# Adapter factors of the first network's gate and up: sums by single sequences inside tile 1, rows spread through DRAM

## The chip, the cores and the metric

The kernel runs on one core of a Trainium2 chip. Its time is the device time of one launch in microseconds; lower is better. The profile is of one execution.

## The reference

Tokens x are 8 sequences of 128 tokens with 512 features, all in float32. Each sequence picks its own low-rank adapters (rank 16) by an index. Cut to what matters:

```python
# first network
gate = x @ W_gate.T + (x @ A_gate[ids].T) @ B_gate[ids].T * 0.5     # 512 -> 1376
up   = x @ W_up.T   + (x @ A_up[ids].T)   @ B_up[ids].T   * 0.5
act  = silu(gate) * up
cond = act @ W_down.T + (act @ A_down[ids].T) @ B_down[ids].T * 0.5  # 1376 -> 512
x = x + ffn0(cond)      # 512 -> 1792 -> 512, weights w * (su @ sv) of rank 4
# second network
y = x @ W.T + b + (x @ A1[ids1]) @ B1[ids1] * 2
x = x + ffn1(y)         # 512 -> 1792 -> 512, int4 weights with scales
```

The change concerns the products x @ A_gate[ids].T and x @ A_up[ids].T, called t below: for each sequence 16 gate rows and 16 up rows of 128 tokens.

## The kernel before, in words

Features lie on the 128 partitions; HK = 4 blocks of 128 features make up 512, and the 1024 tokens are two chunks c of 512 (CH = 2), each of four sequences. A float32 operand is split into a rounded high part (ScalarE, `_hi`) and the rest (VectorE, `lo`), and each block product is three matmuls of 128 x 512: high by high, high by low, low by high (`sums`, L2355 to L2357). The gate/up weights of the first network come in 11 tiles of 128 outputs. Tiles 0 and 1 are computed plainly (`plain_base(t, c)`: gate bank, then up bank, 12 matmuls each), tiles from 2 on with seven products over sums of blocks.

Every engine has its program written out in one order, tied together by semaphores. `first_tiles` is TensorE's start: 12 warm-up matmuls (`WARM`, L2783), tile 0 in both chunks, the adapter sums, tile 1 in both chunks, and then the adapter products of both tiles (`gate_up_adapters`, L2365), followed by the tiles from 2 on.

The adapter sums (L2374) work on pairs of sequences: for each chunk and block, four matmuls of 32 weight columns by 256 tokens, one on each quarter of the array's columns (two pairs for gate, two for up). Their weights are the factors of two sequences side by side, reordered on ScalarE from a_gu_raw into a_gu (L1578). Half of each result belongs to the wrong sequence; VectorE multiplies by seg_mask to clear it (L2221, into gated). ScalarE writes the high part into quarter 0 of t_rows (`hi_of_t`), VectorE the low part into quarter 2 (`lo_of_t`), and SP copies each to the quarter behind it inside SBUF (`copy_t`, L863 and L865; semaphore t_copied). t_rows then has four quarters of 32 rows (high, high, low, low), and one matmul against b_rows (the B factors as high, low, high, low) adds the adapters to a tile.

b_rows comes by DMA through DRAM: SP stores the split B factors (`store_first`, L802, into b_split) and spreads them with four transfers per group of tiles (`spread_b`, L810). spread_b(0) serves tiles 0 and 1, spread_b(1) tiles 2 and 3. SP also issues nearly all weight loads in its fixed order: after x come the adapter factors of four sequences, tile 1's weights (load(gu_a, 1), L781), B factors, load(gu_a, 2), down factors, store_first(0), copy_t(0), spread_b(0), copy_t(1), store_first(1), load(gu_a, 3), spread_b(1). GpSimd issues the loads of the other four sequences, then waits, and later computes the block sums of tile 3 (`cond_sums(3)`, L1026 on).

Of the kernel before, what the change touches and what calls it, by code (L numbers as in the profile page):

```python
# [6 lines left out]
F32 = mybir.dt.float32  # L7
F32R = mybir.dt.float32r
# [57 lines left out]
WARM = 12  # L66
# [127 lines left out]
def adaln_ffn(nc, d, out):  # L194
# [7 lines left out]
    with ExitStack() as ctx:  # L202
# [116 lines left out]

        gate_sum = place("gate_sum", [P, 4, TOK], F32, at["h"])  # L320
# [19 lines left out]
        a_gu = place("a_gu", [P, HK, 2, NB, R], F32, at["act_lo"] + 8 * KB)  # L340
# [35 lines left out]
        a_gu_ready = sem("a_gu_ready")  # L376
# [3 lines left out]
        t_copied = [sem(f"t_copied{c}") for c in range(CH)]  # L380
# [164 lines left out]


# [83 lines left out]
        start = [("w", 0)] + [("x", 0, k) for k in range(HK)] + [("w", 1)] + [("x", 1, k) for k in range(HK)]  # L630
# [130 lines left out]

        block = ctx.enter_context(nc.Block())
# [3 lines left out]
        def _(sp):  # L766
# [60 lines left out]

            for n, item in enumerate(start):
# [8 lines left out]

            sp.wait_ge(ids_in[0], 16)
            indices = {b: sequence(sp, b) for b in range(BC, NB)}
            for b in range(BC, NB):  # L840
                load_a_gu(sp, b, indices[b])
            gu_a, down_a, gu_b, down_b, gu_c, down_c = phases[:6]
            load(gu_a, 1)
            for b in range(BC, NB):
                load_b(sp, b, indices[b], 0, b_in[b // BC])
# [14 lines left out]
            def copy_t(c):  # L860

                sp.wait_ge(t_hi_rows, c + 1)
                sp.dma_start(t_rows[quarter(1), :, chunk(c)].bitcast(F32), t_rows[quarter(0), :, chunk(c)].bitcast(F32)).then_inc(t_copied[c], 16)  # L863
                sp.wait_ge(t_lo_rows_done, c + 1)
                sp.dma_start(t_rows[quarter(3), :, chunk(c)].bitcast(F32), t_rows[quarter(2), :, chunk(c)].bitcast(F32)).then_inc(t_copied[c], 16)  # L865

            store_first(0)
            copy_t(0)
            sp.wait_ge(b_stored[0], 16 * 2)
            spread_b(0)  # L870
            copy_t(1)
# [126 lines left out]
        def _(pool):  # L998
# [12 lines left out]
            for b in range(BC):  # L1011
                load_a_gu(pool, b, indices[b])
            for b in range(BC):
                load_b(pool, b, indices[b], 0, b_in[b // BC])
            pool.wait_ge(start_lo, len(start))
            for b in range(BC):
                load_a_dn(pool, b, indices[b])

# [180 lines left out]
        def _(act):  # L1199
# [44 lines left out]
            def hi_of_t(c, nets):  # L1244

                n = nets * RB
                act.wait_ge(t_masked, (0 if nets == 2 else CH + 1) + c + 1)
# [308 lines left out]
            def small_t(ph):  # L1556
# [4 lines left out]
                for c in range(CH):  # L1561
                    hi_of_t(c, 1)
# [22 lines left out]
            for c in range(CH):  # L1585
                hi_of_t(c, 2)
# [1341 lines left out]
```

## Time and profile before

| what | value |
|---|---|
| median of 3 runs | 606.76 us (606.46 to 607.78) |
| profiled execution | 606.15 us, span 604.5 us |
| TensorE busy | 99% of the span, 2904 matmuls |
| VectorE, ScalarE, GpSimd busy | 78%, 49%, 48% |
| DMA | 56.06 MB, mean 93 GB/s |

The span runs from the first to the last instruction; the runs are some 1.6 us longer than the span. PE is TensorE (PEld its weight loads), DVE is VectorE, ACT ScalarE, POOL GpSimd, SPq the queue of SP, which issues DMAs. In a timeline a line gives the start, the time covered, engine, line of the kernel, operation, what is written from what, the shape and how many instructions are merged; in brackets stands the idle time ahead of it and what ended it. Matmul ends are modelled and overlap the next start; the distance of starts is the pace.

### The profile page before, as it was taken

How to read it: one execution, taken by the hardware profiler on the slowest of the kernel's cores; microseconds unless marked ns; L12 is line 12 of the kernel's file. 1: busy time of each engine (PE TensorE's matmuls, PEld its weight loads, DVE VectorE, ACT ScalarE, POOL GpSimd, SP SyncE). 2: the span in 40 equal slices, each digit the busy share in tenths (PEclk: the TensorE clock that was granted, in tenths of full speed). 3: DMA queues.
4: the chain of work that ended last, by engine and by line, in shares of the span. 5: the costliest groups of instructions: out<-in, count | busy, mean ns of one | idle time of the engine just before them, and what ended most of it. 6: DMA issues, size and time to landing. Idle time of an engine off the chain costs nothing.

```text
span 604.5 us, 8075 instructions
## 1 busy us (share of the span) xinstructions
PE 599.7 (99%) x2904; PEld 491.9 (81%) x2904; DVE 469.7 (78%) x572; ACT 295.3 (49%) x413; POOL 292.7 (48%) x219
## 2 busy tenths in 40 slices
PE   8999999999999999999999999999999999999997
PEld 7787887878778888888888878888788888888886
DVE  6797757757778999873459877645879998999987
ACT  5865224323443445441124445334658886478860
POOL 6135334324434055831034586520005889958897
PEclk9999999999999999999999999999999999999999
DMA  8896472541171215212121200342232221322203
GB/s 255 220 227 180 148 170 65 131 130 28 53 207 37 71 35 166 69 31 66 35 71 35 70 30 31 84 83 84 61 101 78 77 69 36 109 67 75 75 7 139
DMA packets 30475, 56.06 MB, mean 93 GB/s; under 512 B 10468, under 2 KB 14532, under 8 KB 30052
## 3 DMA queue, kind: packets, MB, share of 16 engines
q1 hardware_dynamic: 28932, 53.05, 30.7%
q0 software_dynamic: 1216, 1.98, 1.5%
q8 instruction: 23, 0.38, 0.3%
q10 hardware_dynamic: 288, 0.52, 0.2%
q14 instruction: 16, 0.13, 0.1%
HBM read 48.44 MB, written 6.06 MB: 90 GB/s over the span
## 4 chain that ended last, share of the span: by engine, by line
PE 99%; DVE 0%; issue 0%
PE ps_down L2355 7%; PE ps_down L2356 7%; PE ps_down L2357 7%; PE ps_gate L2458 3%; PE ps_gate L2639 3%; PE ps_gate L2638 3%; PE ps_up L2638 3%; PE ps_gate L2459 3%; PE ps_gate L2460 3%; PE ps_up L2639 3%; PE ps_m L2638 3%; PE ps_down L2638 3%; PE ps_m L2639 3%; PE ps_down L2639 3%; PE ps_up L2458 3%; PE ps_up L2459 2%
## 5 line engine op out<-in xcount | busy, mean ns | idle before, releaser
L1144 POOL TENSOR_TENSOR up_sum<-up_sum,up_more 128x1024 f32<-128x1024 f32 x14 | 33.7, 2409 | 62.6 <-DVE up_more L1926 62.6
L2355 PE MATMUL ps_down<-act_hi,w_hi 128*128 128x512 f32 x112 | 43.9, 392 | 0.0
L2356 PE MATMUL ps_down<-act_lo,w_hi 128*128 128x512 f32 x112 | 43.6, 390 | 0.0
L2357 PE MATMUL ps_down<-act_hi,w_lo 128*128 128x512 f32 x112 | 43.6, 389 | 0.0
L1026 POOL TENSOR_TENSOR cond_total<-w_raw 128x512 f32<-128x512 f32 x8 | 10.5, 1310 | 60.4 <-DMA w_raw<-in_cond_gu 36.3
L1691 DVE TENSOR_TENSOR w_lo<-w_total,w_hi 128x512 fp32r<-128x512 f32 (+1 forms) x28 | 28.8, 1030 | 13.3 <-ACT w_hi L1462 12.6
L1926 DVE SCALAR_TENSOR_TENSOR gate_sum<-ps_up,s_group,gate_sum 128x1024 f32<-128x1024 f32 x28 | 35.8, 1279 | 3.8 <-PE ps_up L2639 3.7
L1102 POOL TENSOR_TENSOR act_lo<-up,act_hi 128x512 fp32r<-128x512 f32 x14 | 18.1, 1295 | 39.1 <-ACT act_hi L1468 39.1
L1156 POOL TENSOR_TENSOR act_lo<-gate_sum,act_hi 128x1024 fp32r<-128x1024 f32 x14 | 33.7, 2413 | 6.3 <-DVE gate_sum L1934 6.3
L1462 ACT ACTIVATE w_hi<-w_total 128x512 fp32r<-128x512 f32 (+1 forms) x28 | 20.7, 738 | 28.8 <-POOL w_total L1089 19.4
L1036 POOL TENSOR_TENSOR act_lo<-cond_out,act_hi 128x512 fp32r<-128x512 f32 (+1 forms) x14 | 19.1, 1389 | 28.9 <-ACT act_hi L1303 28.9
L2181 DVE TENSOR_TENSOR xp<-xp,ps_down 128x512 f32<-128x512 f32 x16 | 11.0, 685 | 27.4 <-PE ps_down L2357 27.4
L2458 PE MATMUL ps_gate<-x_hi,w_hi 128*128 128x512 f32 x80 | 31.9, 398 | 0.0
L2459 PE MATMUL ps_gate<-x_lo,w_hi 128*128 128x512 f32 x80 | 31.2, 390 | 0.0
L2460 PE MATMUL ps_gate<-x_hi,w_lo 128*128 128x512 f32 x80 | 31.2, 390 | 0.0
L1084 POOL TENSOR_TENSOR w_total<-w_raw 128x512 f32<-128x512 f32 x7 | 9.5, 1354 | 42.9 <-DVE w_raw L1698 33.6
L1151 POOL TENSOR_TENSOR gate_sum<-gate_sum,up_sum 128x512 f32<-128x512 f32 (+1 forms) x14 | 20.4, 1459 | 11.7 <-ACT gate_sum L1382 11.7
L2458 PE MATMUL ps_up<-x_hi,w_hi 128*128 128x512 f32 x66 | 26.0, 394 | 0.0
L2459 PE MATMUL ps_up<-x_lo,w_hi 128*128 128x512 f32 x66 | 25.8, 390 | 0.0
L2460 PE MATMUL ps_up<-x_hi,w_lo 128*128 128x512 f32 x66 | 25.7, 389 | 0.0
L2357 PEld LDWEIGHTS ps_down<-act_hi,w_lo 128*128 128x128 f32 x112 | 21.0, 188 | 4.5
L2355 PEld LDWEIGHTS ps_down<-act_hi,w_hi 128*128 128x128 f32 x112 | 21.0, 188 | 4.3
(413 smaller groups left out, 2031.5 us busy)
## 6 DMA issues: line engine op xcount, KB each, us to landing
w_int<-in_ffn_gu SPq DMA_DIRECT2D x14, 512.0 KB, 3.5
w_raw<-in_ffn_gu SPq DMA_DIRECT2D x10, 512.0 KB, 4.1
w_raw<-in_cond_gu SPq DMA_DIRECT2D x9, 512.0 KB, 5.9
w_raw<-in_ffn_dn SPq DMA_DIRECT2D x8, 448.0 KB, 3.2
w_int<-in_ffn_dn SPq DMA_DIRECT2D x8, 448.0 KB, 3.2
b_rows<-b_split SPq DMA_DIRECT2D x12, 256.0 KB, 4.6
xp<-in_x SPq DMA_DIRECT2D x8, 256.0 KB, 4.9
w_raw_third<-in_ffn_gu SPq DMA_DIRECT2D x4, 512.0 KB, 4.0
```

The lines of the kernel that those rows point to most:

```text
L1144: nc.gpsimd.tensor_tensor(up_sum[:, u % 3, :], up_sum[:, u % 3, :], up_more[:, u % 2, :], ALU.add).then_inc(up_done, 1)
L1156: nc.gpsimd.tensor_tensor(act_lo[:, j, :], gate_sum[:, u % 4, :], act_hi[:, j, :].bitcast(F32), ALU.subtract).then_inc(unit_ready, 1)
L1691: return nc.vector.tensor_tensor(out_, value, hi.bitcast(F32), ALU.subtract)
L1926: return nc.vector.scalar_tensor_tensor(out=here, in0=group_bank(g), scalar=group_scale(g), in1=here, op0=ALU.mult, op1=ALU.add)
L2355: nc.tensor.matmul(ps[:, :], weights_hi[:, cols], rhs_hi(k), start=start and n == 0, stop=False)
L2356: nc.tensor.matmul(ps[:, :], weights_hi[:, cols], rhs_lo(k), start=False, stop=False)
L2357: last = nc.tensor.matmul(ps[:, :], weights_lo[:, cols], rhs_hi(k), start=False, stop=stop and n == len(ks) - 1)
L2458: nc.tensor.matmul(bank[:, :], w7_hi[s][:, cols], x_hi[n][:, k, :], start=not more and k == 0, stop=False, skip_group_check=more)
L2459: nc.tensor.matmul(bank[:, :], w7_hi[s][:, cols], x_lo[n][:, k, :], start=False, stop=False, skip_group_check=more)
L2460: last = nc.tensor.matmul(bank[:, :], w7_lo[s][:, cols], x_hi[n][:, k, :], start=False, stop=k == 1, skip_group_check=more)
L2638: nc.tensor.matmul(bank[:, chunk(c)], weights, hi[:, chunk(c)], start=True, stop=False)
L2639: last = nc.tensor.matmul(bank[:, chunk(c)], weights, lo[:, chunk(c)], start=False, stop=True)
```

## The change

In words:
- The sums go by single sequences: four matmuls of 32 weight columns (16 gate, 16 up) by 128 tokens for each chunk and block, read from a_gu_raw as loaded. The reordering a_gu, the mask product on gated and the writes into t_rows by ScalarE and VectorE go for this use.
- The sums stand in tile 1, between the gate and the up bank of chunk 0 (`between`).
- ScalarE takes the high part of a whole result (128 x 128) and VectorE the low part. GpSimd stores the high halves to DRAM (t_split) and spreads them with 8 transfers of 16 partitions into t_rows; SP does the same with the low halves, its 8 transfers behind spread_b(0). VectorE clears t_rows at the start, since the transfers write only each sequence's own places. All adapter products wait for all 16 transfers.
- Tile 0's first chunk alternates gate and up by block, and the up weights are loaded third, not sixth. Nine warm-up matmuls, not twelve.
- Tile 1's weights are loaded ahead of the adapter factors, and the B factors ahead of the A factors.
- On ScalarE and VectorE the x sums for tile 2 (`cond_x_high`, `cond_x_sum`) change places with the work around them. Some semaphore counts of later stages shift, with no work changed there.

```diff
-WARM = 12
+WARM = 9
...
+        t_first_hi, t_first_lo = (place(f"t_first_{part}", [P, CH, P], F32R, at[home]) for part, home in (("hi", "t_hi"), ("lo", "gated")))
+        t_split = nc.dram_tensor("t_split", (2, NB, 2, R, P), F32, kind="Internal").ap()
...
-        start = [("w", 0)] + [("x", 0, k) for k in range(HK)] + [("w", 1)] + [("x", 1, k) for k in range(HK)]
+        start = [("w", 0), ("x", 0, 0), ("w", 1)] + [("x", 0, k) for k in range(1, HK)] + [("x", 1, k) for k in range(HK)]
...
+        def store_t(eng, half, c):
+
+            value = (t_first_hi, t_first_lo)[half][:, c, :]
+            eng.dma_start(t_split[half, c * BC:(c + 1) * BC].rearrange("s g r n -> (s g r) n"), value.bitcast(F32)).then_inc(t_stored[half], 16)
+
+        def spread_t(eng, half):
+
+            for q in (2 * half, 2 * half + 1):
+                for odd in range(2):
+                    rows = t_rows[q * PR + odd * R:q * PR + (odd + 1) * R, :, :].rearrange("r g (p e n) -> r g p e n", e=2, n=P)
+                    values = t_split[half].rearrange("(p e) g r n -> e g r p n", e=2)[odd]
+                    for g in range(2):
+                        eng.dma_start(rows[:, g, :, odd, :].bitcast(F32), values[g]).then_inc(t_copied[half], 16)
...
+            load(gu_a, 1)
             sp.wait_ge(ids_in[0], 16)
             indices = {b: sequence(sp, b) for b in range(BC, NB)}
             for b in range(BC, NB):
+                load_b(sp, b, indices[b], 0, b_in[b // BC])
+            for b in range(BC, NB):
                 load_a_gu(sp, b, indices[b])
-            gu_a, down_a, gu_b, down_b, gu_c, down_c = phases[:6]
-            load(gu_a, 1)
-            for b in range(BC, NB):
-                load_b(sp, b, indices[b], 0, b_in[b // BC])
...
-            def copy_t(c):
-
-                sp.wait_ge(t_hi_rows, c + 1)
-                sp.dma_start(t_rows[quarter(1), :, chunk(c)].bitcast(F32), t_rows[quarter(0), :, chunk(c)].bitcast(F32)).then_inc(t_copied[c], 16)
-                sp.wait_ge(t_lo_rows_done, c + 1)
-                sp.dma_start(t_rows[quarter(3), :, chunk(c)].bitcast(F32), t_rows[quarter(2), :, chunk(c)].bitcast(F32)).then_inc(t_copied[c], 16)
-
             store_first(0)
-            copy_t(0)
+            for c in range(CH):
+                sp.wait_ge(t_first_lo_done, c + 1)
+                store_t(sp, 1, c)
             sp.wait_ge(b_stored[0], 16 * 2)
             spread_b(0)
-            copy_t(1)
+            sp.wait_ge(t_zero, 1)
+            sp.wait_ge(t_stored[1], 16 * CH)
+            spread_t(sp, 1)
...
+                load_b(pool, b, indices[b], 0, b_in[b // BC])
+            for b in range(BC):
                 load_a_gu(pool, b, indices[b])
-            for b in range(BC):
-                load_b(pool, b, indices[b], 0, b_in[b // BC])
             pool.wait_ge(start_lo, len(start))
             for b in range(BC):
                 load_a_dn(pool, b, indices[b])
+
+            for c in range(CH):
+                pool.wait_ge(t_first_hi_done, c + 1)
+                store_t(pool, 0, c)
+            pool.wait_ge(t_zero, 1)
+            pool.wait_ge(t_stored[0], 16 * CH)
+            spread_t(pool, 0)
...
-            def hi_of_t(c, nets):
-
-                n = nets * RB
-                act.wait_ge(t_masked, (0 if nets == 2 else CH + 1) + c + 1)
-                nc.scalar.activation(t_hi[0:n, c, 0:PT], gated[0:n, c, 0:PT], ACT.Copy).then_inc(t_hi_done, 1)
-                for g in range(nets):
-                    for half in range(2):
-                        for row in (0, 1) if nets == 1 else (0,):
-                            last = nc.scalar.activation(t_rows[quarter(row), g, pair_tokens(2 * c + half)],
-                                                        gated[quarter(2 * g + half), c, 0:PT], ACT.Copy)
+            def hi_of_first_t(c):
+
+                act.wait_ge(t_sums, c + 1)
+                nc.scalar.activation(t_first_hi[:, c, :], ps_m[:, sample_sums(c)], ACT.Copy, scale=0.5).then_inc(t_first_hi_done, 1)
...
-                act.wait_ge(a_gu_in[c], 16 * BC)
-                for g in range(2):
-                    nc.scalar.activation(a_gu[:, :, g, c * BC:(c + 1) * BC, :], a_gu_raw[:, c * BC:(c + 1) * BC, :].rearrange(
-                        "p b (k g r) -> p g k b r", g=2, r=R)[:, g], ACT.Copy).then_inc(a_gu_ready, 1)
...
-            cond_x_high(3)
+            for n in (3, 1):
+                cond_x_high(n)
             for c in range(CH):
-                hi_of_t(c, 2)
-            for n in (1, 4):
-                cond_x_high(n)
+                hi_of_first_t(c)
+            cond_x_high(4)
...
+            def lo_of_first_t(c):
+
+                dve.wait_ge(t_first_hi_done, c + 1)
+                nc.vector.scalar_tensor_tensor(out=t_first_lo[:, c, :], in0=ps_m[:, sample_sums(c)], scalar=0.5, in1=t_first_hi[:, c, :].bitcast(F32),
+                                               op0=ALU.mult, op1=ALU.subtract).then_inc(t_first_lo_done, 1)
...
+            nc.vector.memset(t_rows[:, :, :].bitcast(F32), 0.0).then_inc(t_zero, 1)
...
-            for n in (3, 1, 4):
-                cond_x_sum(n)
+            cond_x_sum(3)
             dve.wait_ge(w_hi_done, 1)
             lo(plain_lo[1][:, :], w_raw[:, 1, :], plain_hi[1][:, :]).then_inc(w_ready, 1)
             for n in range(2):
                 lo_of_b_first(n)
-            dve.wait_ge(mask_ready, 4)
+            for n in (1, 4):
+                cond_x_sum(n)
             for c in range(CH):
-                dve.wait_ge(t_sums, c + 1)
-                nc.vector.scalar_tensor_tensor(out=gated[:, c, 0:PT], in0=ps_m[:, pair_sums(c)], scalar=0.5, in1=seg_mask[:, :],
-                                               op0=ALU.mult, op1=ALU.mult).then_inc(t_masked, 1)
-                lo_of_t(c, 2)
+                lo_of_first_t(c)
...
-                pe.wait_ge(t_copied[c], 16 * 2)
+                for half in range(2):
+                    pe.wait_ge(t_copied[half], 16 * 8)
...
+                if (t, c) == (0, 0):
+                    for k in range(HK):
+                        for g in range(2):
+                            last = part(g, range(k, k + 1))
+                else:
+                    for g in range(2):
+                        last = part(g, range(HK))
+                        if g == 0:
+                            between()
...
+            def first_t():
+
+                for c in range(CH):
+                    pe.wait_ge(a_gu_in[c], 16 * BC)
+                    for k in range(HK):
+                        for q in range(4):
+                            sample = BC * c + q
+                            last = nc.tensor.matmul(ps_m[quarter(q), sample_sums(c)], a_gu_raw[:, sample, k * 2 * R:(k + 1) * 2 * R],
+                                                    xp[:, k, sample * P:(sample + 1) * P], start=k == 0, stop=k == HK - 1)
+                    last.then_inc(t_sums, 1)
+
             def first_tiles():
 
                 for c in range(CH):
                     plain_base(0, c)
-                for c in range(CH):
-                    pe.wait_ge(a_gu_ready, 2 * (c + 1))
-                    for k in range(HK):
-                        last = pair_products(c, lambda q: pair_factors(a_gu[:, k, q // 2], c, q), lambda q: xp[:, k, pair_tokens(2 * c + q % 2)],
-                                             k == 0, k == HK - 1)
-                    last.then_inc(t_sums, 1)
                 pe.wait_ge(w_ready, 1)
-                plain_base(1, 0)
-                pe.wait_ge(t_masked, CH)
+                plain_base(1, 0, first_t)
+                pe.wait_ge(t_first_lo_done, CH)
```

## Rows read from the trace of the kernel before

**Rows 1.** Page, busy time, and the chain that ended last by engine.

```profile
PE 599.7 (99%) x2904; PEld 491.9 (81%) x2904; DVE 469.7 (78%) x572; ACT 295.3 (49%) x413; POOL 292.7 (48%) x219
...
PE 99%; DVE 0%; issue 0%
```

**Rows 2.** All waits of TensorE over the span: total us, times, longest.

```profile
PE ps_m L2783 <- DVE warm L2203: 1.7, 1, 1.7
```

**Rows 3.** Timeline of TensorE, 0 to 45 us: start, us, work.

```profile
1.65 5.49 PE L2783 MATMUL ps_m<-warm 128*128 128x512 f32 x12 [1.65 <-DVE warm L2203]
6.94 0.63 PE L2355 MATMUL ps_down<-h_hi,plain_hi 128*128 128x512 f32 x1
...
7.80 0.43 PE L2357 MATMUL ps_down<-h_hi,plain_lo 128*128 128x512 f32 x1
8.06 0.39 PE L2355 MATMUL ps_down<-h_hi,plain_hi 128*128 128x512 f32 x1
...
18.36 3.66 PE L2374 MATMUL ps_m<-xp,a_gu 128*32 128x256 f32 x64
21.95 0.50 PE L2355 MATMUL ps_gate<-h_hi,plain_hi 128*128 128x512 f32 x1
...
32.96 0.64 PE L2365 MATMUL ps_down<-t_rows,b_rows 128*128 128x256 f32 x4
...
43.06 0.40 PE L2365 MATMUL ps_down<-t_rows,b_rows 128*128 128x256 f32 x2
```

**Rows 4.** Timeline of VectorE, 0 to 60 us.

```profile
1.11 0.48 DVE L2203 MEMSET warm<- 128x512 f32 x1 [1.11 <-PEq L2921]
4.29 0.78 DVE L1691 TENSOR_TENSOR plain_lo<-w_raw,plain_hi 128x512 fp32r<-128x512 f32 x1 [2.69 <-ACT plain_hi L1570]
5.19 0.69 DVE L1691 TENSOR_TENSOR h_lo<-xp,h_hi 128x512 fp32r<-128x512 f32 x1
6.83 2.03 DVE L1691 TENSOR_TENSOR h_lo<-xp,h_hi 128x512 fp32r<-128x512 f32 x3 [0.95 <-ACT h_hi L1574]
...
18.38 1.23 DVE L1691 TENSOR_TENSOR plain_lo<-w_raw,plain_hi 128x1024 fp32r<-128x1024 f32 x1 [1.96 <-ACT plain_hi L1581]
```

**Rows 5.** Timeline of ScalarE, 0 to 45 us.

```profile
15.14 1.34 ACT L1578 ACTIVATE a_gu<-a_gu_raw 128x256 f32<-128x256 f32 x4 [2.86 <-DMA a_gu_raw<-in_a_gu]
...
21.39 0.42 ACT L1248 ACTIVATE t_hi<-gated 128x256 fp32r<-128x256 f32 x1 [0.23 <-DVE gated L2221]
```

**Rows 6.** The sums' weight loads by line: duration ns min/median/max.

```profile
L2374 PEld LDWEIGHTS ps_m<-xp,a_gu x64: 106/110/110, 18.4 to 21.4; 128*32 128x32 f32 x64
```

**Rows 7.** Timeline of SP's DMA queue, 0 to 60 us: issues.

```profile
10.54 0.43 SPq L781 DMA_DIRECT2D w_raw<-in_cond_gu  x1
...
24.88 2.02 SPq L810 DMA_DIRECT2D b_rows<-b_split  x4
...
27.59 0.59 SPq L865 DMA_DIRECT2D t_rows<-t_rows  x1
...
29.34 0.48 SPq L781 DMA_DIRECT2D w_raw<-in_cond_gu  x1
34.07 1.74 SPq L810 DMA_DIRECT2D b_rows<-b_split  x4
```

**Rows 8.** Tile t_rows, its four DMA copies, issue to landing.

```profile
DMA to landing us min/median/max: 2.3/3.8/5.4
```

**Rows 9.** DMA issues, 0 to 60 us and whole span: KB, us to landing.

```profile
factor_split<-factor_lo SPq DMA_DIRECT2D x3, 36.0 KB, 1.8
...
b_raw<-in_b POOLq DMA_DIRECT2D x8, 32.0 KB, 2.7
```

**Rows 10.** Timeline of GpSimd, 0 to 70 us.

```profile
35.50 1.29 POOL L1026 TENSOR_TENSOR cond_total<-w_raw 128x512 f32<-128x512 f32 x1 [16.75 <-DMA w_raw<-in_cond_gu]
...
38.69 1.94 POOL L760 DMA_DIRECT2D b_raw<-in_b  x4
```

**Rows 11.** Window 23 to 25 us: busy by engine, PEclk, DMA share, GB/s.

```profile
23.00:25.00 2.00, 2.00 (x10) 1.67 (x9) 1.46 (x5) 1.35 (x4) 0.00 (x0) 1.00 0.14 43
```

## What I predict, before the change was run

> **What bounds the kernel now.** I read the page first. TensorE is busy for 99% of the span, and the chain that ended last runs through it for 99% [rows 1]. The list of waits, asked for TensorE alone, has one entry: the 1.7 us before the warm-up matmuls [rows 2]. So no wait can be taken away here. The time falls only if TensorE gets less to do, or does real work where it warms up, and every gap that a change opens in its queue is paid in full. The next view is the timeline of each engine over the first 45 us, because the diff touches nothing later but semaphore counts. Twelve warm-up matmuls begin at 1.65 us, the first real one starts at 6.94, the adapter sums run from 18.36 to 21.95, the adapter products of tiles 0 and 1 start at 32.96, and tile 2's at 43.06 [rows 3]. From 21.95 to 32.96 lie 48 matmuls, so one costs 0.229 us. The matmul at 7.80 still takes 0.43 us and the one at 8.06 is at full pace, so TensorE runs at 1.2 GHz up to about 7.85 us, after 6.2 us of unbroken work, and at 2.4 GHz from there (granted clock 1.00 in a later window [rows 11]). The number that decides the case is 32.96 and what it becomes.
>
> **Part 1, the start.** VectorE has the first block of x split at 5.19 + 0.69 = 5.88 us [rows 4], but TensorE is still warming up until 6.94. Nine warm-up matmuls of 0.44 end at 5.6, so real work starts at 5.95 (I take 0.06 for a semaphore, as between the end of the memset, 1.11 + 0.48, and 1.65 [rows 3, 4]). Three matmuls at half pace end at 7.2. The next three need the up weights, which now are the third load. Today's third load is x's second block, the same 256 KB, and VectorE starts on its split at 6.83 [rows 4], so the up weights are ready at 7.5 and TensorE goes on at 7.6. The clock should rise near 7.85 as before; it has then done 4 matmuls, not 2.5. The remaining 44 of tile 0 at 0.229 end at 18.0, against 18.3: a gain of 0.3 us. The later x blocks come 0.7 us apart, each feeding 1.4 us of work, so none is late. The new memset of t_rows is four times the old one, at most 4 x 0.48 = 1.9 us from 1.6 on, and VectorE's next work is later than 3.5 [rows 4]: nothing.
>
> **Part 2, the sums.** Today 64 matmuls take 3.59 us: 16 rounds of four column quarters, 0.22 each [rows 3]. The new ones have half the columns, which gives 0.11 a round; a 32-column weight load takes 0.11 too [rows 6]. So 0.11 to 0.12 a round, 1.9 us in all with its two joints; the upper bound is that the round stays at 0.22 and nothing is gained. I take 1.9 (both parts of a round halve or fit), a gain of 1.7. The mask product, the four fp32 reorderings on ScalarE (15.14, 1.34 us [rows 5]) and the eight 32-row copies go; the engines that did them are off the path, so this counts only through readiness.
>
> **Part 3, the order.** Tile 1's gate half now runs ahead of the sums, from 18.0 to 20.7. Its weights are split at 18.38 + 1.23 = 19.6 today [rows 4], which would be a stall of 1.6 us; but the load now goes out right behind the x loads and not at 10.54 [rows 7]. Eight splits of 0.7 after 6.83 keep VectorE to about 13, one x sum and the split itself follow, so it is ready near 15.4. The adapter factors are issued some 2 us later than today, when ScalarE had them at 15.14 [rows 5]; they have until 20.8. Both at nothing. The sums then run 20.8 to 22.7, and 36 matmuls (the up half and the second chunk) of 8.25 us follow: TensorE reaches the adapter products at 30.95. That is 2.0 us before 32.96, and is the most that the change can give.
>
> **Part 4, the rows.** Today SP copies t_rows inside SBUF, the last copy issued at 27.59 [rows 7]; with up to 5.4 us to land [rows 8] it is there at 33.0, just as TensorE arrives. The new way has two transfers in a row for each half, and every TensorE use waits for all of both. I add up the high half, which goes through GpSimd:
> 1. second chunk's sums readable at 22.8, ScalarE 0.3 (0.42 for 256 elements [rows 5]): 23.2.
> 2. store of 64 KB. Bounds: 1.8 us to land for SP's stores of 36 KB, 5.4 for the t_rows copies among other traffic [rows 8, 9]; GpSimd's loads of 32 KB take 2.7 [rows 9]. I take 2.8: 26.0.
> 3. eight issues. GpSimd's four of 16 partitions take 1.94, so 0.49 each [rows 10]; the eighth starts at 26.0 + 7 x 0.49 = 29.5.
> 4. its landing, 2.7 by the row of 32 KB, with 0.7 added because SP's rows are in flight: 3.4, so 32.9. Bounds 1.8 and 5.4.
> The low half goes through SP: VectorE has it at 23.45, the stores are out at 23.9, then spread_b(0) with four issues of 2.02 in all [rows 7] keeps SP until 25.9, the stores have landed by 26.3, eight issues at about 0.47 (the b_rows issues' pitch) put the last at 29.6, behind spread_b(0)'s 1 MB on the same rings, and 2.3 to 4 to land [rows 8] gives 31.9 to 33.6, middle 32.7. So the adapter products wait for t_copied until 32.9 plus a semaphore: 32.95. TensorE stands idle for 2 us in front of them, and the gain of parts 1 and 2 is gone.
>
> The Trainium skill, "DMA: Bandwidth & Descriptors", section "Anatomy of one DMA — SWDGE (gpsimd) path", gives a GpSimd DMA 2.0 us plus its bytes over 436 GB/s. By that the store takes 2.15 and the last spread 2.1, and as an estimate the high half is there at about 30.95, with nothing left to wait for; the same section warns that a DMA which writes to HBM can be slow to report, which speaks against this change. No row of before has a store issued by GpSimd.
>
> **Part 5, what queues behind.** On SP store_first(1), load(gu_a, 3) and spread_b(1) stand behind the eight issues: the load leaves at about 31.2, not 29.34, and spread_b(1) at about 36, not 34.07 [rows 7]. GpSimd's sums for tile 3 start at 35.5 today when that load lands [rows 10], and the pieces are read from 40.9 on, so 2 us later is still in time. spread_b(1), its last issue near 37.3, lands by 42.6 if it takes no more than 5.3, and is needed at 43.06 [rows 3]: in time by half a microsecond. At nothing, but the cover is thin: another 1 us late costs 0.5.
>
> **Sum.** Start -0.3, sums -1.7, new wait +2.0: 32.95 against 32.96, a change of 0.0 in the profiled execution, whose own time is 606.15 us with a span of 604.5. The median of the runs shown is 606.76, 0.6 above it, and I forecast from that: 606.8.
>
> **Rivals.**
> A. The rows land early. If store and spread both land in the 1.8 us of SP's small stores, the high half is there at 23.2 + 1.8 + 3.4 + 1.8 = 30.2, the low half near 31, and all of parts 1 and 2 stays: 606.76 - 2.0 = 604.8. For it: the DMA engines were only 14% busy between 23 and 25 us [rows 11]. Against it: spread_b(0) now fills just this stretch. The skill's formula in part 4 is this case. 0.26.
> B. The rows land late, the case on the other side. If the last spread takes 5.4 us as the t_rows copies did among spread_b(0)'s packets, it lands at 29.5 + 5.4 = 34.9: +1.95, so 608.7. It decides from a landing of 34.2 on. For it: that row; against it: those copies had a store of 512 KB and a 512 KB load right behind. 0.15.
> C. The sums don't shorten: rounds stay at 0.22, the chain starts 1.7 later and ends at 34.6: 608.4. 0.04.
> D. TensorE's clock falls in the new 2 us idle stretch, or rises late because the start now has two small gaps. The profile shows a stay of 6.2 us at 1.2 GHz before it rose; that again costs 3.1 us: 609.9. Rows of before show no fall at all, since nothing idles. The skill, "TensorE: Matmul & The Clock Gate", says idleness throttles the array again; no row here shows for which gaps. 0.04.
> E. spread_b(1) is late by 2 us or more and tile 2 stalls: +1.5, 608.3. 0.03.
>
> **How the numbers follow.** 0.2% is 1.2 us, about what a measurement of this kernel can tell from no change. The forecast (0.48) has the rows landing between 31.8 and 34.1, which is 605.6 to 608.0: same. A is faster (0.26); B, C, D, E are slower (0.26). The range takes in A's and B's values, 604.7 to 608.8, and leaves out D and the tails.
>
> **What would show it.** Right: first real matmul near 5.95; sums of 1.8 to 2.0 us starting at 20.8; a gap in TensorE of about 2 us before the first adapter product near 33, released by a t_rows transfer; the b_rows wait of tile 2 absent. If the gap is missing and the products start near 31, A. If the sums take over 3 us, C. Matmuls of 0.43 us after the gap, D. A wait at about 43 us, E. The step I trust least is the landing of GpSimd's store and last spread; 1 us of error in it moves the result by 1 us.

## The result: 0.7% slower, and the profile after

| | before | after |
|---|---|---|
| median of 6 runs, us | 606.61 (606.19 to 607.78) | 610.39 (609.63 to 612.5) |
| span of the profiled execution, us | 604.5 | 608.7 |
| mean granted clock | 1.000 | 0.994 |

The ratio is 1.0067, interval [1.0049, 1.0086]: 3.8 us slower, where 606.8 us was forecast with 608.8 as the upper end. The ratios here and below leave out two executions at a mean granted clock of 0.66 and 0.85, one of the kernel before (856.58 us) and one of the kernel with later traffic held back (666.97 us). Of the ways laid out beforehand it is B and D together: the rows land late, and TensorE's clock falls in the gap that this opens.

The list of waits of TensorE had one entry [rows 2]; it now has three.

```profile
PE ps_down L2390 <- DMA t_rows<-t_split: 3.7, 1, 3.7
PE ps_m L2826 <- DVE warm L2229: 1.7, 1, 1.7
PE ps_down L2380 <- DVE h_lo L1712: 0.7, 1, 0.7
```

TensorE's timeline, over the first 45 us:

```profile
1.65 4.21 PE L2826 MATMUL ps_m<-warm 128*128 128x512 f32 x9 [1.65 <-DVE warm L2229]
6.52 0.50 PE L2380 MATMUL ps_down<-h_hi,plain_hi 128*128 128x512 f32 x1 [0.66 <-DVE h_lo L1712]
...
20.59 1.95 PE L2546 MATMUL ps_m<-xp,a_gu_raw 128*32 128x128 f32 x64
22.47 0.50 PE L2380 MATMUL ps_gate<-h_hi,plain_hi 128*128 128x512 f32 x1
...
34.63 1.23 PE L2390 MATMUL ps_down<-t_rows,b_rows 128*128 128x256 f32 x4 [3.71 <-DMA t_rows<-t_split]
35.66 1.05 PE L2390 MATMUL ps_up<-t_rows,b_rows 128*128 128x256 f32 x4
...
38.22 0.63 PE L2602 MATMUL ps_up<-h_hi,cond_hi 128*128 128x512 f32 x1
...
39.92 0.42 PE L2603 MATMUL ps_up<-h_lo,cond_hi 128*128 128x512 f32 x1
```

The sums start at 20.59 and last 1.9 us. The last plain matmul starts at 30.53, so TensorE is at the adapters at 30.75 and starts on them at 34.63, 1.67 later than before. What follows costs more too: four adapter products took 0.64 before [rows 3] and take 1.05, and the matmuls behind them are spaced 0.43 us apart until 39.9. The windows show why (columns as in [rows 11]: length, busy by engine, PEclk, DMA share, GB/s).

```profile
22.00:24.00 2.00, 2.00 (x27) 1.54 (x20) 1.38 (x4) 1.40 (x4) 1.08 (x2) 1.00 0.39 118
24.00:26.00 2.00, 2.00 (x10) 1.65 (x9) 2.00 (x4) 2.00 (x4) 0.37 (x1) 1.00 0.64 165
26.00:28.00 2.00, 2.00 (x10) 1.68 (x9) 2.00 (x3) 0.99 (x2) 2.00 (x5) 1.00 1.04 239
...
32.00:34.00 2.00, 0.00 (x0) 0.00 (x0) 0.00 (x0) 0.00 (x0) 0.00 (x0) 0.78 1.11 261
...
36.00:39.90 3.90, 3.90 (x16) 3.54 (x15) 2.75 (x4) 1.86 (x4) 3.35 (x4) 0.50 1.00 227
39.90:43.00 3.10, 3.10 (x15) 2.52 (x14) 0.93 (x2) 2.38 (x3) 1.76 (x4) 0.99 1.18 194
```

The granted clock falls at 33.1 us, while TensorE is idle, and stays at half, 1.2 GHz, until 39.96. The price can be read without adding matmuls up: from the first adapter product to the end of the span it was 604.5 - 32.96 = 571.54 us, and is 608.7 - 34.63 = 574.07. So 2.5 us for the clock and 1.67 for the later start, together the 4.2 us between the spans. The 2.5 us are those of the profiled execution, whose mean clock is 0.994; of the six runs three show 0.994 and three 0.997, so the stretch at half clock isn't equally long in all.

The DMA engines were 14% busy at 23 to 25 us before [rows 11]; from 26 us on they are now full. The two queues of the rows, and how long the rows take to land (tile t_rows, as [rows 8]):

```profile
L780 POOL DMA_DIRECT2D t_rows<-t_split x8: 512/512/528, 25.6 to 29.2; - x8
L780 SPq DMA_DIRECT2D t_rows<-t_split x8: 362/426/435, 25.9 to 29.1; - x8
...
DMA to landing us min/median/max: 5.2/5.5/5.7
```

SP's queue just ahead of it (its timeline, answering [rows 7]):

```profile
22.36 1.53 SPq L771 DMA_DIRECT2D t_split<-t_first_lo  x2
23.93 1.87 SPq L830 DMA_DIRECT2D b_rows<-b_split  x4
25.92 3.65 SPq L780 DMA_DIRECT2D t_rows<-t_split  x8
```

The packet records of the trace, counted per microsecond by their start, give the reason. The last three columns are numbers of packets, with the size of one in brackets:

```
after, us     KB moved   b_rows (SP, 2 KB)   rows (SP, 512 B)   rows (GpSimd, 2 KB)
25 to 26      190          95                  -                  -
26 to 27      240         120                  -                  -
27 to 28      226         113                  -                  -
28 to 29      228         111                  -                  3
29 to 30      202          71                 44                 19
30 to 31      212           -                223                 48
31 to 32      211           -                222                 46
```

The rows were issued from 25.6 us on, half of them on GpSimd's own queue. The first packet of GpSimd's moves at 28.4, the first of SP's at 29.6, when b_rows' 1 MB is nearly through; the last ones end at 32.4, and TensorE sees them at 34.6.

The trace of the kernel before already had both cases. Of its four copies of t_rows [rows 8], two were issued ahead of spread_b(0), at 23.4 and 24.3, and two behind it, at 27.0 and 27.6 (tile t_rows over 23 to 25 us and over 26.5 to 28.5):

```profile
DMA to landing us min/median/max: 2.3/2.4/2.5
DMA to landing us min/median/max: 5.2/5.3/5.4
```

### The profile page after: what moved, and what is told of

Its sections match the earlier page's. It is cut to its first block, busy times and chain, and to the rows that moved or that the text cites. A ratio compares the mean times of both kernels' runs of the same rounds, so it can differ in the third digit from the quotient of the medians.

```text
span 608.7 us, 8086 instructions
## 1 busy us (share of the span) xinstructions
PE 599.5 (98%) x2901; PEld 492.1 (81%) x2901; DVE 470.8 (77%) x565; ACT 290.9 (48%) x401; POOL 298.5 (49%) x229
## 4 chain that ended last, share of the span: by engine, by line
PE 96%; DMA 2%; POOL 1%; issue 0%; DVE 0%; ACT 0%; SPq 0%; POOLq 0%
PE ps_down L2380 7%; PE ps_down L2381 7%; PE ps_down L2382 7%; PE ps_gate L2483 3%; PE ps_gate L2681 3%; PE ps_gate L2682 3%; PE ps_up L2681 3%; PE ps_gate L2484 3%; PE ps_gate L2485 3%; PE ps_up L2682 3%; PE ps_down L2682 3%; PE ps_m L2681 3%; PE ps_down L2681 3%; PE ps_m L2682 3%; PE ps_up L2483 3%; PE ps_up L2484 2%
## 5 line engine op out<-in xcount | busy, mean ns | idle before, releaser
L2483 PE MATMUL ps_gate<-x_hi,w_hi 128*128 128x512 f32 x80 | 31.9, 398 | 0.0
L1367 ACT ACTIVATE cond_out<-cond_out 128x512 f32<-128x512 f32 (+1 forms) x9 | 5.7, 633 | 39.7 <-DVE cond_out L1907 39.7
```

Of the source, the lines that this page charges most:

```text
L2483: nc.tensor.matmul(bank[:, :], w7_hi[s][:, cols], x_hi[n][:, k, :], start=not more and k == 0, stop=False, skip_group_check=more)
```

## The experiments

Each ratio is to the kernel before on the same chip; "sums to adapters" runs from the first adapter sum to the first adapter product, 14.6 us before and 14.04 after. TensorE's own work in it is 10.15 us in all the changed kernels (20.59 to 30.75).

**Only the start: WARM 9, the new load order, gate and up by turns in tile 0.** On the kernel before:

```diff
-WARM = 12
+WARM = 9
-        start = [("w", 0)] + [("x", 0, k) for k in range(HK)] + [("w", 1)] + ...
+        start = [("w", 0), ("x", 0, 0), ("w", 1)] + [("x", 0, k) for k in range(1, HK)] + ...
```

> The kernel before with the start of the change alone: nine warm-up matmuls, the up weights loaded third, gate and up alternating by block in tile 0's first chunk. Sums, rows and copies as before. If the start is worth what its rows say, the first real matmul comes near 6.0 to 6.5 us instead of 6.94, everything behind it shifts by the same amount, since the copies of the rows are issued earlier too: 606.2 (0.4 faster). Rival: the copies landed at about 33.0 for reasons of DMA traffic and stay there; then TensorE waits in front of the adapter products and the time stays at 606.6.

607.29 us, 1.0002 [0.9992, 1.0012]. The sums start at 17.80, not 18.36, and the adapters at 32.52, 0.44 earlier. That lead is gone by tile 2's products, which start at 43.16 (before: 43.06). The copies of t_rows land at 32.59 and 33.12, when TensorE is already in the adapter products of tiles 0 and 1, and these take 2.18 us in all instead of 1.91; 0.3 more is lost about 41.5, where TensorE's weight load (41.67) follows VectorE's h_lo (ready at 41.56). Further on comes a wait that before didn't have:

```profile
PE ps_gate L2365 <- DVE cond_e L1874: 0.4, 1, 0.4
```

So this part alone neither gains nor costs, and the rival of the expectation, rows that don't come sooner, holds in part.

**The clock alone.** After, with 16 matmuls of zeros added into a bank behind tile 1:

```diff
                 plain_base(1, 1)
+                pe.wait_ge(fill_ready, 1)
+                for n in range(16):
+                    nc.tensor.matmul(ps_down[0][:, :], fill_zero[:, 0:P], fill_zero[:, :], start=False, stop=False, ...)
```

> The changed kernel with 16 matmuls of zeros (3.7 us at full pace) between tile 1 and its adapter products, where TensorE stands idle for 3.7 us; they add zero to a sum and change no result. If the fall of the clock costs what the pace shows (12 to 13 half-pace matmul times from 34.6 to 40.0, 2.7 us), the time is 607.7 and no matmul is slow after the adapter products. Rival: the clock falls for another reason or the slow stretch hides a second wait; then 610.4 stays.

609.38 us, 1.0043 [1.0028, 1.0058]. The clock holds in all five runs (0.999 to 1.000), and four products take 0.64 again:

```profile
36.00:40.00 4.00, 4.00 (x25) 3.51 (x24) 2.48 (x4) 3.01 (x6) 2.94 (x3) 1.00 0.89 204
```

From the first adapter product (35.19) to the end of the span (606.9) it is 571.7 us, as before, against 574.07: the clock's price is 2.4 us. The rows landed in 5.9 and the adapters start 0.56 later than after, so 1.8 of it is left in the span. The rest of the loss is the rows. 607.7 was expected; of the difference 0.56 is the later rows, and the rest is open (the profiled execution, at 608.54, is the fastest of the five).

**b_rows behind the rows.** After, with spread_b(0) moved:

```diff
-            spread_b(0)
             sp.wait_ge(t_zero, 1)
             sp.wait_ge(t_stored[1], 16 * CH)
             spread_t(sp, 1)
+            spread_b(0)
```

> The changed kernel with SP's spread_b(0) (four transfers of 256 KB) behind its eight transfers of t_rows instead of ahead of them. If the rows landed 5.5 us after issue because they queued behind 1 MB of b_rows, they now land in 2.3 to 3 us, the last of GpSimd's at about 32. If 32 KB in pieces of 512 bytes to 16 partitions are slow by themselves, they still take over 5 us. The time itself should not gain: b_rows then lands near 33 to 35 and TensorE waits for that: 609 to 611.

613.06 us, 1.0099 [1.0081, 1.0117]. The rows' landing drops from 5.5 to 2.0, and the adapters now wait for b_rows:

```profile
PE ps_down L2390 <- DMA b_rows<-b_split: 5.5, 1, 5.5
```

```profile
t_rows<-t_split SPq DMA_DIRECT2D x8, 32.0 KB, 1.9
t_rows<-t_split POOLq DMA_DIRECT2D x8, 32.0 KB, 2.1
```

This shows that b_rows' 1 MB ahead is what makes a landing of 2 us one of 5.5, on GpSimd's queue too, which it never passes through. The medians hide that the same thing happened once more inside this run: GpSimd's last two transfers were issued at 31.02 and 31.52, just after SP had begun on b_rows (30.87, then one of 256 KB every 0.47 us), and took 4.05 and 5.09 us, where the six before them took 2.0 to 2.2.

The Trainium skill, "DMA: Bandwidth & Descriptors", section "Anatomy of one DMA — SWDGE (gpsimd) path", gives a fixed 2.0 us and the bytes over 436 GB/s, as an estimate 2.1 us for 32 KB. With nothing ahead GpSimd's median agrees; with 1 MB ahead (5.5) it is off by 3.4 us.

**Later traffic held back.** After, with store_first(1) and load(gu_a, 3) waiting for the rows:

```diff
             spread_t(sp, 1)
+            for half in range(2):
+                sp.wait_ge(t_copied[half], 16 * 8)
             store_first(1)
```

> The changed kernel with SP holding the second B store and tile 3's weight load until all t_rows transfers have landed. If traffic that is issued behind the last rows slows them (GpSimd's queue shares the engines with SP's), the rows land 1 to 2 us earlier, near 33, and the clock falls less or not at all: 607 to 609.5. If only what is ahead counts, the rows still land at 34.5 and the time is 610.4 or more, since the held load may then be late for tile 3.

612.18 us (median of three), 1.0075 [1.0053, 1.0097]; landing 5.6, the wait 3.9. The time itself can't be compared with after's, since the profiled execution lost 2.4 us in waits for VectorE's h_lo before the sums, but the landing can: what is issued behind the last row has no part in it.

**b_rows earlier.** After, with store_first(0) and spread_b(0) ahead of SP's stores of t_split, and half of SP's a_dn loads behind:

```diff
             store_first(0)
+            for b in range(BC + 2, NB):
+                load_a_dn(sp, b, indices[b])
+            sp.wait_ge(b_stored[0], 16 * 2)
+            spread_b(0)
             for c in range(CH):
                 sp.wait_ge(t_first_lo_done, c + 1)
```

> The changed kernel with SP storing the first half of the split B factors as soon as it is there (about 17.4 and 18.1 us, four of its down-factor loads behind it) and issuing spread_b(0) at about 21.6 us, ahead of its stores of the rows' low halves. If the rows landed late because the 1 MB of b_rows stood ahead of them, that megabyte is now through at about 26.5 and the rows issued from 26 on land in 2 to 3.5 us; the low stores leave 1 us later, so the last row comes near 32.5, the gap shrinks from 3.7 to about 2 us and the clock stays up: 606.5 to 607.5. If GpSimd's and SP's many small transfers are the limit, the gap and the slow clock stay: 610.

610.9 us, 1.0064 [1.0047, 1.0081]. The rows land in 2.0 and 1.9, but the stores take 3.2 and 4.2 instead of 2.2 and 2.1, and SP issues its rows from 30.81 to 34.4 instead of 25.92 to 29.6. Sums to adapters 13.94, and the time misses the 606.5 to 607.5 expected: the megabyte delays whichever of the two transfers comes behind it. Part of that is SP's own time: with four issues of b_rows in front, its low stores leave at 26.07, 4.1 us after the sums' start, against 1.8 in after.

**Three queues.** As the last one, with the 16 row transfers over ScalarE (6), GpSimd (6) and SP (4), and the stores on ScalarE (high) and GpSimd (low):

```diff
+            act.wait_ge(t_stored[0], 16 * CH)
+            spread_t(act, [(0, 0), (0, 1)], "act")
+            act.wait_ge(t_stored[1], 16 * CH)
+            spread_t(act, [(3, 0)], "act")
```

> As the kernel before this one, and the 16 row transfers split over three issuing engines, six on ScalarE, six on GpSimd, four on SP; ScalarE stores its own high halves, GpSimd the low ones. The last issue moves from 29.2 to about 28.3 and no store waits behind another. If issue and queueing are the whole of it, the rows are there near 30.7, TensorE arrives at 30.75 and hardly waits, and the adapter products start up to 2 us earlier than in the kernel before: 604.8 to 605.3. Rival: ScalarE's issues push its other work, or later transfers (tile 3's weights, spread_b(1)) become late for a TensorE that is 2 us ahead, and the gain is given back in front of tiles 2 or 3: 606 to 607.

613.42 us (608.65 to 615.36, the lowest at a mean clock of 1.000), 1.0087 [1.0056, 1.0118]. Far from the 605 expected, and inconclusive for the queues: the first x block came late (landed at 6.46, in after at 5.09), the first real matmul started at 7.90, the clock rose only at 13.95, and TensorE waited 4.0 in front of the adapters. One thing it shows all the same. The stores of 512 KB by store_first(1), issued by SP at 32.85 and 33.32, now come ahead of the last rows. The rows issued before them land in 1.8 to 2.5 us; ScalarE's last, issued at 33.20, takes 4.0, and GpSimd's last two, at 33.50 and 34.00, take 3.3 and 4.8. So it need not be b_rows: another large transfer from another queue goes with the same delay.

**Twelve warm-up matmuls.** After, with:

```diff
-WARM = 9
+WARM = 12
```

> The changed kernel with the twelve warm-up matmuls of before. If nine leave a gap before the first real matmul that sometimes keeps the clock at 1.2 GHz for some us longer (two of the six kernels with nine rose only after 11 and 14 us), twelve give up to 0.5 us later starts but a lower and narrower time, 609.5 to 610.2 with a spread under 1 us. Rival: the start has no share in the loss, and the time is 610.4 to 610.8 with the spread of before (2.9 us).

611.19 us, 1.0071 [1.0058, 1.0085]; landing 5.4, wait 3.7, sums to adapters 14.0. The nine warm-up matmuls have no share in the loss; the spread was 2.0 us, not the 1 us expected of them.

**b_rows between the stores and the rows, three queues.** With 12 warm-up matmuls, SP's a_dn loads divided as in "b_rows earlier", t_split's high half stored by ScalarE, spread_b(0) behind SP's stores, and store_first(1) held until ScalarE's rows are there:

```diff
             for c in range(CH):
                 sp.wait_ge(t_first_lo_done, c + 1)
                 store_t(sp, 1, c)
             sp.wait_ge(b_stored[0], 16 * 2)
             spread_b(0)
-            spread_t(sp, 1)
+            spread_t(sp, [(2, 0), (2, 1)], "sp")
+            sp.wait_ge(t_by[0][1], 16 * 6)
             store_first(1)
```

> Twelve warm-up matmuls; high halves stored by ScalarE, low halves by SP, spread_b(0) issued right behind both stores (its 4 us of transfer then run while the stores are being reported), the 16 row transfers split over ScalarE, GpSimd and SP (6, 6, 4), the second B store held until ScalarE's transfers have landed. If the DMA engines serve in order of issue whatever the queue, and nothing but b_rows stands ahead, the rows are there at about 32.2 and the gap is 1.2 us: 605.8 to 606.3, the clock stays up. If issue by three engines doesn't help and the rows again come 14 us after the start of the sums, 608 to 610.

610.47 us, 1.0065 [1.0052, 1.0077]. The rows are issued by 28.4, 1.3 us sooner than after, and land in 6.1 to 6.5: sooner issued, they only queue longer. All the rearranging, the third queue with it, buys 0.3 us of sums to adapters (13.73), where a wait of 1.2 was expected and 3.4 is there.

**Half of b_rows ahead.** The last kernel with b_rows loaded by single tiles: tile 0's 512 KB ahead of the rows, tile 1's behind them.

```diff
-B_LOADS = ((0, 2), (2, 4), (4, 7), (7, 9), (9, 11))
+B_LOADS = ((0, 1), (1, 2), (2, 4), (4, 7), (7, 9), (9, 11))
             spread_t(sp, [(2, 0), (2, 1)], "sp")
+            spread_b(1)
```

> As the kernel before this one with b_rows of tile 0 (512 KB) ahead of the row transfers and tile 1's behind them, so only half stands ahead of the rows. If the amount ahead sets the landing, the rows come 1 to 2 us earlier than there, TensorE waits 0 to 0.5 us and then perhaps 0.5 for tile 1's b_rows: 605.0 to 605.6, below the kernel before the change. If the landing doesn't follow the amount ahead, the time is that of the kernel before this one.

607.54 us (605.75 to 609.77, 12 runs), 1.0015 [1.0003, 1.0026], not the 605.0 to 605.6 expected. The mean clock is 1.000 in the profiled execution; the two slowest of the twelve runs, 608.74 and 609.77, show 0.997.

```profile
PE ps_down L2402 <- DMA t_rows<-t_split: 1.6, 1, 1.6
```

```profile
t_rows<-t_split ACTq DMA_DIRECT2D x6, 32.0 KB, 3.6
t_rows<-t_split POOLq DMA_DIRECT2D x6, 32.0 KB, 3.8
```

Halving the data ahead takes 2.5 us off the median landing and 2.2 off that of the last transfer, for which TensorE waits (6.6 to 4.4). It also changes the size of b_rows' packets, from 2 KB to 1 KB, with about the same bytes per us; that this has no part was not tried. Sums to adapters is 11.93: of the 3.6 us that the last kernel had above TensorE's own 10.15, 1.8 are gone, and with the shorter gap the clock stays in ten of twelve runs.

Here b_rows of tiles 2 and 3 became late. It landed at 44.57, and TensorE's weight load for tile 2's adapters, 0.11 us behind that, had 0.51 us of idle time ahead of it (the view names no releaser):

```profile
44.68 0.30 PEld L2402 LDWEIGHTS ps_down<-t_rows,b_rows 128*128 128x128 f32 x2 [0.51 <-issue]
```

The product itself starts at 44.71, 0.28 later than the pace of the matmuls before it would have had it.

**The old start under it.** The same with the first load order and without the turns of gate and up in tile 0 (twelve warm-up matmuls as there).

> The kernel of the halves experiment (512 KB of b_rows ahead of the rows, tile 1's behind them), with the load order and the first products of the kernel before (no gate and up alternation in tile 0, its twelve warm products). If the small waits at the start of the halves experiment came from the new load order, they are gone: 606.0 to 606.8 us, with a narrower spread than before. The rival theory, that the start has no part in it because everything up to the adapters ends with the rows' landing, expects the halves experiment's 607.5 again, with a wait of 1.5 to 2 us ahead of the adapters.

607.28 us (606.19 to 608.72, 11 runs), 1.0012 [1.0003, 1.0021]. Sums to adapters is 11.48. Its profiled execution, the second fastest of its runs, has a span of 604.6, and the adapters start at 32.29, 0.67 ahead of before. Yet the span is before's within 0.1. TensorE's weight loads and VectorE show where the lead goes:

```profile
45.26 0.19 PEld L2615 LDWEIGHTS ps_gate<-h_hi,cond_hi 128*128 128x128 f32 x1 [0.17 <-DVE cond_lo L1724]
```

```profile
40.49 2.32 DVE L1832 SCALAR_TENSOR_TENSOR h_lo<-cond_x_total,h_hi 128x1024 fp32r<-128x1024 f32 x1
...
44.53 0.68 DVE L1724 TENSOR_TENSOR cond_lo<-cond_total,cond_hi 128x512 fp32r<-128x512 f32 x1
```

The piece is ready at 45.21, and TensorE takes it at 45.26; before, the same one was ready at 44.84 and used at 45.39. TensorE loses 0.13 us there, and 0.26 at 42.7, where its weight load (42.92) follows the end of the h_lo above (42.81) by 0.11 us. With the first matmul behind each gap, which takes 0.1 longer, the lead is used up, and the second adapter factor's sums start at 50.95 in both kernels. So behind the adapters stands VectorE with about half a microsecond of cover. b_rows for tile 2 stands right beside it: here it landed at 42.31, and the products that need it started at 42.45.

The small waits at the start didn't go (0.6 for h_lo before 7.65), the time is above the 606.0 to 606.8 expected, and the spread of 2.5 us is narrower than the 4.0 of the kernel above, not than the 1.3 of the kernel before.

**A quarter of b_rows ahead.** The last kernel with two of tile 0's four transfers (256 KB) ahead of the rows:

```diff
-            spread_b(0)
+            spread_b(0, (0, 1))
             sp.wait_ge(t_zero, 1)
...
+            spread_b(0, (2, 3))
             spread_b(1)
```

> The same kernel with only two of tile 0's four b_rows transfers (256 KB) ahead of the rows, the other two and tile 1's behind them. If the amount of b_rows that stands ahead on the DMA engines sets the rows' landing (5.5 us with 1 MB, 3.7 us with 512 KB, 1.9 to 2.1 us with none), 256 KB gives 2.5 to 3 us, a time from the sums' start to the adapters near 11 us and a wait of 0.5 to 1 us, perhaps already for b_rows: 605.3 to 606.3 us. The rival, that the b_rows put behind become the late ones, expects a wait for b_rows ahead of the adapters as long as the one removed or longer, and a time no lower than that of the kernel with 512 KB ahead.

607.22 us (606.21 to 607.96, 11 runs), 1.0012 [1.0003, 1.0021]. A miss: the landing is 3.3 to 4.0 (medians of the three queues), where the last kernel had 3.8 to 4.2, and the wait is 1.5, where that had 1.1.

```profile
PE ps_down L2403 <- DMA t_rows<-t_split: 1.5, 1, 1.5
```

Sums to adapters is 11.80, no shorter than with the half. The last rows are issued at 27.7 to 28.2, but GpSimd's packets end only at 30.7, for those of b_rows that were put behind, issued from 26.69 on, now move among them; 1.8 us more pass until TensorE sees the rows. With all of b_rows behind (the third experiment) SP's rows moved their last packets, at 32.0, just as b_rows moved its first, at 31.9. So less data ahead of the first rows brings the landing down to about 3.7 and not below; that b_rows issued among the last rows sets the rest is read from the packets and wasn't tried.

## Why the prediction was wrong, step by step

**Part 1, the start.** Predicted a gain of 0.3; the sums started 0.2 earlier than forecast (20.59 against 20.8), but by another way: TensorE waited 0.66 for VectorE's h_lo, so real work started at 6.52, not 5.95, and the clock rose at 5.8 and not at 7.85. So the forecast of this part came out by luck. Alone the part gave 0.44 us at the adapters and nothing at the end.

**Part 2, the sums.** Right: 1.9 us, a gain of 1.7. Rival C didn't happen.

**Part 3, the order.** Right: no wait for tile 1's weights or for the factors; TensorE is at the adapters at 30.75 (predicted 30.95; the 0.2 is the start's).

**Part 4, the rows.** Items 1 to 3 came out a little better than written: the high half ready at 22.9, the stores landed in 2.2 (I took 2.8), the eighth issue at 29.2 (29.5). **The step that failed is item 4, the landing of the last spread: 3.4 us predicted, 5.5 measured** (median; 5.4 for the very last), and the same for the low half, 2.3 to 4 predicted behind spread_b(0)'s megabyte, 5.4 measured. I had put that megabyte on SP's rings alone, and priced GpSimd's half by a row of 32 KB with 0.7 for its neighbour. The 5.4 of [rows 8] I took for a far bound; it was what both copies issued behind spread_b(0) took, and the 2.3 what those ahead of it took. The experiments showed that the megabyte stands ahead of every queue (2.0 us with it behind, 5.5 with it ahead, 3.7 with half of it). With after's own rates the chain adds up: 1 MB at some 220 KB per us lasts from 25 to 29.7, the rows' 512 KB until 32.4 (partly among it), and 2.2 us to the report make 34.6. Rival B had the landing (5.4, 34.9) for just this cause, with 0.15.

**Rival D.** This is the second step that failed: the clock stood in the sum at nothing, and its fall, with a chance of 0.04, as a case apart. No run waits just the 2 us foreseen in front of the adapters. The waits of 1.1 to 1.6 us in the profiled executions of the last three experiments left the clock at 1.000, though two other runs of the halves experiment show 0.997. In the profiled executions of all seven kernels where TensorE waited 3.4 us or more with nothing to do (3.4 with b_rows between, 5.5 with b_rows behind) it fell. What I missed is that B brings D. B's own +1.67 gives 608.4, inside the range; with 2.5 for the clock it is 610.9, past it. So it is the clock that put the time outside the range, and the landing that made the gap for it. The price that D gave, 3.1 us for another stay of 6.2 at half clock, was near: 2.5 for one of 6.8.

**Part 5, what queues behind.** Right in its sum: spread_b(1) was issued at 35.09, its last transfer landed at 42.30 (42.6 written), and no wait at tile 2 appeared (rival E), but TensorE itself was 4 us later by then. Where TensorE came sooner the thin cover showed: a delay of 0.28 in the halves experiment, 0.14 between landing and use in that with the old start. The latter tested what else is behind: there VectorE's pieces are the next bound, at 45 us. So rival A's 604.8 could hardly have been reached either. With its lead of 2.0 tile 2's products would stand at 41.1, and b_rows landed at 42.3; and a lead of 0.67 shrank to nothing by 51 us. What a larger one would leave was not tried.

No version beat the kernel before. The best ones (607.2 to 607.3) are 0.1% above it.

## What to carry to other kernels

A small transfer that TensorE waits for is priced by all bytes issued ahead of it on any queue, divided by what the full DMA engines move (here 220 KB per us), with some 2 us from its last packet until the landing is seen, and not by the landing of a like transfer from a quiet stretch. Splitting the large one so that only what is due first goes ahead was worth 1.8 us here, against 0.3 for issuing from three queues. When a chain ends in a wait of TensorE, price the wait and the clock as one case: here a wait of 3.7 us, 1.67 of it lateness against before, cost 4.2. And before counting on a lead, look one stage further for what has the least slack; here it was 0.5 us of VectorE and, beside it, the next b_rows.

## What the runs showed of the hardware that I had not expected

- Transfers issued on GpSimd's and ScalarE's queues started late and got a small share of the bytes beside 1 MB issued earlier from SP. After: GpSimd's first packet at 28.4 for issues from 25.6 on, 2.8 us, against 1.3 with b_rows behind. With b_rows between: ScalarE's first at 26.9 for issues from 24.8 on, its last at 31.6. From 27 to 28 us of that run ScalarE's queue moved 64 packets of 512 B and SP's 92 of 2 KB: two thirds of SP's packets, but a sixth of its bytes.
- The megabyte ahead lengthens the end of a transfer too. From the last data packet of the rows until the last landing it was 0.4 us where nothing large was ahead (SP's rows with b_rows behind, both queues with b_rows earlier), 2.2 in after, and 1.4 to 2.1 with a half or a quarter of b_rows ahead. With later traffic held back it was still 2.1, with the DMA engines at 0.00 from 36 to 38 us, so it isn't what follows. Why is open.
- The clock rose at very different times at the start, with like warm-ups: 4.5 and 5.8 us in kernels where real work started at 6.3 and 6.5, 11.0 and 13.95 in two with gaps of 1.5 to 2 us before the first real matmuls.
- It fell at different points of the wait: at 33.13 in after, 2.2 us after TensorE ran dry, at 38.33 with b_rows behind, 5.1 after, and with b_rows earlier and with twelve warm-up matmuls only 0.65 and 0.29 us after TensorE had gone on. It stayed at half for 6.8 us in three kernels and 3.4 in four; with twelve warm-up matmuls, one of the four, the stretch from the first adapter product to the end is 573.55 us, against 574.07 in after and 571.54 before.
- One operation of VectorE and one of GpSimd took about twice their time where they met. GpSimd in the kernel with the old start, beside the 2.32 us of VectorE shown there:

```profile
39.40 2.33 POOL L1057 TENSOR_TENSOR cond_total<-w_raw 128x512 f32<-128x512 f32 x1
```

and the same two operations in the kernel before, where they don't meet:

```profile
37.45 1.31 POOL L1029 TENSOR_TENSOR cond_total<-w_raw 128x512 f32<-128x512 f32 x1
```

```profile
41.23 1.21 DVE L1794 SCALAR_TENSOR_TENSOR h_lo<-cond_x_total,h_hi 128x1024 fp32r<-128x1024 f32 x1
```

That they slow each other is what the rows suggest, as if they ran one after the other; it wasn't tried by itself. It isn't so for every pair: in the kernel before GpSimd's 1.31 us contain one of VectorE's operations that reads ps_down (37.89, 0.69 us), and neither took longer.
